# Wide score and maximum products of an attention kernel made by four column tiles of the array

## The reference, cut to what matters

```python
Q, K, V = (proj(Wq), proj(Wk), proj(Wv))            # (2, 16, 2048, 16) each
scores = scale * jnp.einsum('bhtd,bhsd->bhts', Q, kb)
scores = jnp.where(future[None, None], -jnp.inf, scores)
m_new = jnp.maximum(m, jnp.max(scores, axis=-1, keepdims=True))
p = jnp.exp(scores - m_new)
l = corr * l + jnp.sum(p, axis=-1, keepdims=True)
acc = corr * acc + jnp.einsum('bhts,bhsd->bhtd', p, vb)
...
x = _layernorm(x + attention(x))
x = _layernorm(x + quantised_product(x))
```

## Time and profile before

| | us |
|---|---|
| median of three runs (lowest, highest) | 1059.32 (1058.05, 1060.43) |
| the profiled execution's own time | 1061.62 |
| its span | 1059.9 |
| front, to the first score product | 126.4 |
| one of groups 0 to 5 (score product to score product, from the second on) | 104.7 |
| group 6, group 7 | 137.3, 129.1 |
| TensorE busy in the span | 993.2 (94%), 6280 matmuls |
| DVE, ACT, POOL busy | 824.0, 710.9, 263.6 |

### The profile page before, as it was taken

One profiled execution on the slowest core, in us unless ns is written; L12 is line 12 of the kernel. 1 busy time (PEld: TensorE's weight loads), 2 busy tenths in 40 slices (PEclk: granted clock), 3 DMA queues, 4 the chain that ended last, 5 costly groups with the idle time before them and its releaser, 6 DMA issues.

```text
span 1059.9 us, 17207 instructions
## 1 busy us (share of the span) xinstructions
PE 993.2 (94%) x6280; PEld 393.9 (37%) x6280; DVE 824.0 (78%) x1083; ACT 710.9 (67%) x1471; POOL 263.6 (25%) x435
## 2 busy tenths in 40 slices
PE   7999899999999999999999999999999899997972
PEld 5555433333333333333333333333323222443431
DVE  4567667778777787877778778777888987699787
ACT  3444467777777778777878787868656566786730
POOL 3444520112011211121111112110201102555544
PEclk9999989999999999999999999999999999999995
DMA  5567500003010201120112011201120600414501
GB/s 168 173 182 237 165 9 7 7 19 84 6 37 26 77 6 38 31 70 8 37 35 67 7 37 36 69 4 42 36 66 8 138 23 1 124 44 140 154 31 49
DMA packets 71768, 66.20 MB, mean 62 GB/s; under 512 B 15112, under 2 KB 65608, under 8 KB 71684
## 3 DMA queue, kind: packets, MB, share of 16 engines
q1 hardware_dynamic: 71684, 65.10, 22.5%
HBM read 43.25 MB, written 21.35 MB: 61 GB/s over the span
## 4 chain that ended last, share of the span: by engine, by line
PE 81%; DVE 7%; ACT 4%; DMA 3%; issue 2%; SPq 1%; POOL 1%; POOLq 0%; DVEq 0%; ACTq 0%
PE ps_acc L709 24%; PE ps_score L728 21%; PE ps_max L683 21%; PE ps_score L602 5%; DVE block_max L956 4%; ACT PR L908 3%; PE ps_score L609 2%; PE ps_max L686 2%; PE ps_max L783 2%; ACT accS L896 1%; DMA end_slots<-heads_out 1%; PE ps_acc L583 1%; DMA V<-heads_out 1%; PE ps_score L694 1%; DMA row_sums<-accS 1%
## 5 line engine op out<-in xcount | busy, mean ns | idle before, releaser
L956 DVE TENSOR_REDUCE block_max<-ps_max 128x2 f32<-128x1024 f32 (+3 forms) x640 | 657.7, 1062 | 179.8 <-PE ps_max L683 91.1
L908 ACT ACTIVATE PR<-ps_score 128x512 f32<-128x512 f32 (+3 forms) x1280 | 622.1, 538 | 216.5 <-PE ps_score L728 200.9
L728 PE MATMUL ps_score<-QS,KS 99*128 99x512 bf16 (+3 forms) x1280 | 388.9, 352 | 16.8 <-ACT PR L908 13.4
L683 PE MATMUL ps_max<-KS,QS 96*128 96x512 bf16 (+3 forms) x1280 | 357.5, 350 | 14.5 <-DVE block_max L956 12.6
L709 PE MATMUL ps_acc<-PR,VG 128*32 128x512 f32 (+3 forms) x2560 | 303.1, 546 | 0.0
L728 PEld LDWEIGHTS ps_score<-QS,KS 99*128 99x128 bf16 x1280 | 118.3, 97 | 331.1 <-ACT PR L908 218.8
L683 PEld LDWEIGHTS ps_max<-KS,QS 96*128 96x128 bf16 x1280 | 120.5, 98 | 105.8 <-DVE block_max L956 41.2
L1178 POOL TENSOR_SCALAR_AFFINE_SELECT PR<-PR 128x512 f32<-128x512 f32 x128 | 81.4, 636 | 309.5 <-ACT PR L908 309.5
L686 PE MATMUL ps_max<-mask_q,ident_b 128*128 128x128 bf16 x512 | 102.2, 220 | 0.0
L709 PEld LDWEIGHTS ps_acc<-PR,VG 128*32 128x32 f32 x2560 | 50.7, 108 | 97.2 <-ACT PR L908 60.3
L1186 POOL CAST max_parts<-neg_max 16x128 bf16<-16x128 f32 (+1 forms) x31 | 8.8, 285 | 274.4 <-ACT neg_max L891 273.4
(11 more groups left out here) (122 smaller groups left out, 461.5 us busy)
## 6 DMA issues: line engine op xcount, KB each, us to landing
QS<-qparts SPq DMA_DIRECT2D x192, 64.0 KB, 2.4
KS<-kparts SPq DMA_DIRECT2D x192, 64.0 KB, 2.4
qparts<-end_slots SPq DMA_DIRECT2D x16, 384.0 KB, 5.3
kparts<-end_slots SPq DMA_DIRECT2D x16, 384.0 KB, 5.7
PR<-in_L_attn_x SPq DMA_DIRECT2D x8, 512.0 KB, 4.5
heads_out<-accS SPq DMA_DIRECT2D x124, 32.0 KB
end_slots<-in_L_attn_x SPq DMA_DIRECT2D x4, 512.0 KB, 9.9
out_y<-end_slots SPq DMA_DIRECT2D x8, 256.0 KB, 2.1
```

Of the source, the lines that this page charges most:

```text
L683: m = pe.matmul(bank[:, 0:w], QS[0:STACK, p, i // TPC, j, i % TPC * P:i % TPC * P + P], KS[0:STACK, p, b, j, 0:w], start=True, stop=not diag)
L728: pe.matmul(bank[:, 0:CH - s], KS[:, p, kb // TPC, j, kb % TPC * P:kb % TPC * P + P], QS[0:KROWS, p, c, j, s:CH], start=True, stop=True).t ...
L908: act.activation(PR[:, k % 4, j, 0:w], ps_score[:, score_slot(pos), 0:w], ACT.Exp, scale=SCALE).then_inc(s_exp, 1)
L956: dve.tensor_reduce(block_max[:, h * PAIR:h * PAIR + PAIR, i, b], ps_max[:, slot_at:slot_at + PAIR, 0:w], AX.X, ALU.max).then_inc(s_reduce ...
```

## The change

Products of at least 384 columns, other than items on the diagonal, are issued as four matmuls, each with 32 of the 128 stationary columns, which write 32 of the 128 output rows. The contraction rows, the moving operand and its columns are the same for the four; the semaphore is raised by the last. Items on the diagonal, whose mask is a second matmul, and products of 128 and 256 columns are made as before. The planner's cost `FORM` becomes 288 columns and is counted at each passage from one form to the other, for score products, items and values, where before 576 was counted once a step. So the plan's places for items change as well. Nothing else is changed.

```diff
--- before.py
+++ after.py
@@ -106,8 +106,12 @@
         full=[(0, n) for n in range(AHEAD, NI)] + [(1, n) for n in range(NI)],
         last=[])
 
+    QUADS, WIDE = 4, 384
+    QW = P // QUADS
+    in_quads = lambda w, diag=False: w >= WIDE and not diag
+
     LAG, BATCH = 2, 1
-    FORM, LOAD, READ, READ_FROM = 576, 256, 2.5, 340
+    FORM, LOAD, READ, READ_FROM = 288, 256, 2.5, 340
 
     def quota(stream):
 
@@ -117,20 +121,25 @@
         read = lambda m: READ_FROM + READ * ITEM_COLS[m]
 
         def place(pace, early):
-            at, done, free, seen, n, out = 0, 0, [0] * MAX_SLOTS, 0, 0, []
+            at, done, free, seen, n, out, quads = 0, 0, [0] * MAX_SLOTS, 0, 0, [], True
             for k, (c, kb) in enumerate(STEPS):
                 out.append([])
                 for j in range(HG):
-                    at += max(CH - skip(c, kb), LOAD)
+                    at += max(CH - skip(c, kb), LOAD) + FORM * (quads != in_quads(CH - skip(c, kb)))
+                    quads = in_quads(CH - skip(c, kb))
                     if n < len(stream) and free[n % MAX_SLOTS] <= at + early and seen * pace <= at:
-                        at = max(at, free[n % MAX_SLOTS]) + made(stream[n][1])
+                        i, b, w, _ = ITEMS[stream[n][1]]
+                        at = max(at, free[n % MAX_SLOTS]) + made(stream[n][1]) + FORM * (quads != in_quads(w, b == i // TPC))
+                        quads = in_quads(w, b == i // TPC)
                         done = max(done, at) + read(stream[n][1])
                         free[n % MAX_SLOTS] = done
                         seen += read(stream[n][1])
                         n += 1
                     out[k].append(n)
                 if k % BATCH == BATCH - 1:
-                    at += FORM + sum(HG * (CH - skip(*STEPS[k - back])) for back in range(LAG, LAG + BATCH))
+                    at += FORM * (not quads)
+                    quads = True
+                    at += sum(HG * (CH - skip(*STEPS[k - back])) for back in range(LAG, LAG + BATCH))
             return out if n == len(stream) else None
 
         return next(out for early in range(0, 16 * CH, CH // 2) for pace in range(160, -1, -2)
@@ -670,6 +679,16 @@
                         if n == FRONT_TURN:
                             turn_first_maxima()
 
+                def product(bank, w, stack, moving, quads, stop=True):
+
+
+                    if not quads:
+                        return pe.matmul(bank[:, 0:w], stack, moving, start=True, stop=stop)
+                    for t in range(QUADS):
+                        m = pe.matmul(bank[t * QW:t * QW + QW, 0:w], stack[:, t * QW:t * QW + QW], moving,
+                                      start=True, stop=stop)
+                    return m
+
                 def item(q, p, n):
 
                     i, b, w, h = ITEMS[n]
@@ -680,8 +699,8 @@
                     diag = b == i // TPC
                     for t in range(PAIR):
                         bank, j = ps_max[:, n % MAX_SLOTS * PAIR + t, :], h * PAIR + t
-                        m = pe.matmul(bank[:, 0:w], QS[0:STACK, p, i // TPC, j, i % TPC * P:i % TPC * P + P],
-                                      KS[0:STACK, p, b, j, 0:w], start=True, stop=not diag)
+                        m = product(bank, w, QS[0:STACK, p, i // TPC, j, i % TPC * P:i % TPC * P + P],
+                                    KS[0:STACK, p, b, j, 0:w], in_quads(w, diag), stop=not diag)
                         if diag:
                             m = pe.matmul(bank[:, w - P:w], ident_b[:, :], mask_q[:, :], start=False, stop=True)
                     m.then_inc(s_piece, 1)
@@ -725,8 +744,8 @@
                             pos = unit_pos(kind, k, j)
                             at_least(pe, s_exp, score_base(g) + pos - behind(pos) + 1)
                             bank = ps_score[:, score_slot(pos), :]
-                            pe.matmul(bank[:, 0:CH - s], KS[:, p, kb // TPC, j, kb % TPC * P:kb % TPC * P + P],
-                                      QS[0:KROWS, p, c, j, s:CH], start=True, stop=True).then_inc(s_st, 1)
+                            product(bank, CH - s, KS[:, p, kb // TPC, j, kb % TPC * P:kb % TPC * P + P],
+                                    QS[0:KROWS, p, c, j, s:CH], in_quads(CH - s)).then_inc(s_st, 1)
                             while n < QUOTA[kind][k][j]:
                                 on, m = STREAM[kind][n]
                                 item(*groups[on], m)
```

## The result

The changed kernel takes 1077.52 us (median of 4, 1072.45 to 1081.22) against 1059.88 of the kernel before: a ratio of 1.0166, interval 1.0115 to 1.0217. Run again beside fresh runs of the kernel before, it took 1073.22 against 1058.12, 1.0143 (1.0116 to 1.0170). So it is slower, by 1.4 to 1.7%. The forecast was 1077.5. The changed kernel's executions go with their mean granted clock: the first four are 1080.32 and 1081.22 us at 0.978 of full, and 1072.45 and 1074.72 at 0.985; the repetition's four lie at 0.984 to 0.988.

The account below looks back on a forecast made before the run. TensorE was taken to bound the front and groups 0 to 5; added switches less savings on tiled products came to +18 us, 1080 in the profiled execution's terms, 1077.5 us from the median, range 1054 to 1112.

Parts of the forecast that it names:

- What bounds it: Whole kernel: TensorE's added time shows in full in groups 0 to 5, nearly in the front, partly in groups 6 and 7.
- terms of 7.0, 9.0, 1.2 and 1.0: Microseconds added in the front (7.0), groups 0 to 5 together (9.0), group 6 (1.2) and group 7 (1.0).
- The sign named for the front: In the front, TensorE's first pass of an f32 unit behind an item would be near 0.1 us longer.
- The count of switches and their kind: Steady group: 98 passages, 18 more than before, 76 between tiled and whole bf16 products, at 0.12 us each.
- The tiled product at 0.216: Tiled score products in a run of tiled work: 0.216 us against some 0.219 whole, 3 ns saved each.
- The step that failed: Planner's placement of items: new costs move some items by a step, and DVE's pace (83 us of 105) leaves room.
- the forecast of +1.5 a group: Groups 0 to 5: 18 more switches at 0.12 us, +2.16, less 0.67 for 224 tiled products, +1.5 each.
- The dear tiled product (1): Rival on tiled products: open loads or issue make each 20 ns dearer, 36 us over 1792, giving 1108; chance 0.17.
- its part on issue: Within that rival: at 62 ns per matmul a tiled product takes 0.248 us, the kernel about 1125.
- Rival 2: Passages between tiled and whole bf16 work are cheap: faster below 0.09 us each, about 1010 near 0; chance 0.13.
- Rival 3: Column tiles sharing bf16 moving data don't run side by side: two to four times 0.213 us, 1300 up; chance 0.03.
- Rival 4: Whole kernel: new order and absorbed waits cancel the switches, leaving the time within 0.2%; chance 0.05.

Follow-up runs that it names:

- the four corners: Whole or tiled products, each at the items' old or new places; a steady group took 104.7 and 106.2 us whole, 105.2 and 106.4 tiled.
- the tiled kernel at the old places: The changed kernel with its items at the places of the kernel before: 1065.43 us, 1.0082 of the kernel before.
- the masked: The changed kernel with the front whole and diagonal items of 384 and 512 columns tiled with their mask matmuls: 1047.57 us, 0.9914 of the kernel before.
- the all-tiled runs: The changed kernel with every score product, item and mask matmul of the groups tiled, front whole: 1012.24 us, 0.9582 of the kernel before; later runs build on it.

## Why the prediction was right, and where not

**What bounds it: right.** TensorE paces the front and groups 0 to 5, and what it was given showed there: +6.3 us in the front, +1.6 in group 0, +1.7 in each of groups 1 to 5; +1.8 in group 6 and +1.3 from there to the end. That is the 19.6 us between the two spans, against terms of 7.0, 9.0, 1.2 and 1.0, 18 in all. The sign named for the front came too: 0.107 us at the first f32 matmul behind a tiled item.

**The count of switches and their kind: right.** The new gaps stand where tiled and whole bf16 products meet, with 0.12 on the way into whole work and 0.10 on the way back; by the starts a switch is worth 0.10 to 0.107 (98 in a steady group, as counted), where 0.12 was taken, by the row that had the value product on one side. The open first load of 0.024 was in that price.

**The tiled product at 0.216: nearly.** It was to save 3 ns and saves none: starts 0.22 apart and a duration of 383 for 382. The 0.67 us of this term in a steady group came to some 0.4, and from the value product's first load alone.

**The step that failed** is the sentence that the new costs move some items by a step and that DVE's pace leaves room for it, which put the new places at nothing. By the four corners they cost 1.2 to 1.5 us a steady group, and in all some 6 to 10 us (ratios of 1.0091 for 1 with whole products; 1.0143 and 1.0166 for 1.0082 with tiled ones) of the 15 to 18; the tiling with its 16 switches costs 0.2 to 0.5. Sixteen switches should be 1.6 to 1.9 us. Summed over the starts as above, in the tiled kernel at the old places the ordinary gaps fell by 0.6, first loads of the values for the most part, and TensorE's waits from 2.0 to 1.5. That others are ready sooner as its own work grows would explain the waits; it is argued, not shown. The forecast had left both out. So the forecast of +1.5 a group was met by +1.7 through two errors that nearly cancel: tiling priced at thrice what it costs in place, and places at nothing. That the sum came out within 0.1 us is luck: the median lies between two pairs of executions 5.6 us apart, and the repetition gave 1073.22.

**Rivals.** The dear tiled product (1) fell: by the masked and the all-tiled runs, in which some 400 and 1100 more of them ran and the time fell. With it falls its part on issue: the 62 ns per matmul that the Trainium skill's TensorE: Matmul & The Clock Gate gives for a decoder that is off would make four of them 0.25 us, and four with their loads take 0.06. Rival 2 (cheap passage between tiled and whole bf16 work, deciding at 0.09 us) came close in price: 0.09 to 0.12 was measured. Rival 3 fell with the 0.22 us between starts. Rival 4 fell as well: some waits were absorbed, but the new order added more. The Trainium skill's TensorEngine Tiling (Array Packing), Key Properties, has TensorE drained at a change of mode; the trace agrees in that the gaps of 0.09 to 0.12 us stand at changes of form, while no run shows what the engine does in them. The loss of the fast load that Gotcha 2 of the same page of the Trainium skill gives for column tiling costs nothing seen here: a tiled load lasts 95 ns against 98 and lies beneath the products.

**What the change missed.** It was one step short. Leaving the masked items whole inside wide scores costs two switches for each such run of items; tiling those as well gives 0.9914, and all products of the groups 0.9582.

## What to carry to other kernels

If one product of a loop must run in column tiles, count the passages between forms over the real order, not the products: a half-converted loop can have more of them than before, and each passage, in or out, costs 0.1 us here. Convert whole loops, even the narrow products and the masks, since a tiled product took the same time as a whole one here. And when a planner's constants are changed along with the code, run the code at the old places and the places with the old code: here the places cost a steady group more (1.2 to 1.5 us) than the code did (0.2 to 0.5), and the whole kernel about as much (1.0091 against 1.0082).

## What had not been expected of the hardware

- Four matmuls of 32 stationary and 128 moving columns, with their four loads, start again every 0.06 us: eight instructions where the kernel before had two, at the same pace.
- A transpose of 32 f32 columns behind a tiled f32 product, and ahead of a tiled bf16 one, keeps the gap of a passage between forms.
- With all switches but the eight of the transposes gone, a steady group takes 98.0 to 98.1 us in four kernels with two orders of items. By its starts that is 91 us of columns, some 450 gaps of 0.006, the eight switches and some 3.5 us of small waits, of which the trace marks 0.8 to 0.9 as waits on ACT and DVE. Why the two orders come to the same waits stays open.
- In group 0 a stretch at half the granted clock comes in some executions of the same kernel and not in others; with it the group took 109.9 us for 106.0.
